# Experts in pairs: the second product in five whole token tiles instead of four whole and two half ones

## What is computed

```
capacity = max(1, int(N / E * K * CAP_FACTOR))          # 2048 / 32 * 4 * 1.25 = 320
buf = zeros((E + 1, capacity, d)).at[e_s, p_s].set(xf[tok])[:E]
h = silu(einsum('ecd,edh->ech', buf, wg)) * einsum('ecd,edh->ech', buf, wu)     # h: 256 inner
out_e = einsum('ech,ehd->ecd', h, wd)
routed = zeros_like(xf).at[tok].add(out_e[flat_e, pos] * gates)
```

## Time and profile before

| | us |
|---|---|
| median of 3 runs | 1134.17 (1133.24 to 1136.13) |
| span of the profiled execution | 1172.3 |
| second product of the experts (L1143), TensorE busy | 126.5 for the full tiles and half tiles together |
| first product (L1129, L1130), TensorE busy | 96.4 and 89.8 |
| expert stages, first to last pair's start | 150.1 to 287.8 and 998.6 to 1136.3 |

### The profile page before, as it was taken

How to read it: one execution, slowest core, us unless ns; L and a number is a source line. 1 busy time by engine, 2 the same in 40 slices (tenths; PEclk the granted TensorE clock), 3 DMA queues, 4 the chain that set the end, 5 groups by cost and what they waited for, 6 DMA issues and landing times.

```text
span 1172.3 us, 17171 instructions
## 1 busy us (share of the span) xinstructions
PE 972.9 (83%) x5887; PEld 752.4 (64%) x5887; DVE 548.8 (47%) x1503; ACT 356.1 (30%) x701; POOL 365.8 (31%) x550
## 2 busy tenths in 40 slices
PE   2305699999198999999999999999999653999994
PEld 1203366666134888979888498887999632666663
DVE  7533244444536674727273556362712541444444
ACT  2100122222023335343432443434353210222222
POOL 2736435555100311111110011444421073355551
PEclk9998899999579999999999999999999775999997
DMA  9400234453400000000000000101000002344435
GB/s 362 166 24 27 58 93 142 146 164 99 147 18 0 19 1 19 1 19 1 19 1 1 0 20 1 37 20 38 19 1 1 28 27 58 105 142 147 153 96 183
DMA packets 79285, 76.31 MB, mean 65 GB/s; under 512 B 10409, under 2 KB 69947, under 8 KB 78454
## 3 DMA queue, kind: packets, MB, share of 16 engines
q1 hardware_dynamic: 70006, 63.15, 17.3%
q0 software_dynamic: 9216, 12.33, 3.1%
HBM read 48.13 MB, written 30.21 MB: 67 GB/s over the span
## 4 chain that ended last, share of the span: by engine, by line
PE 72%; DVE 10%; issue 7%; another core or an unknown queue 6%; DMA 2%; ACT 2%; SPq 1%; POOL 1%; DVEq 0%; POOLq 0%; ACTq 0%
PE PS L1232 22%; PE PS L1143 8%; PE PS L1212 7%; PE PS L1129 6%; PE PS L1194 6%; PE PS L1130 5%; PE PS L1174 3%; PE PS L1283 3%; PE PS L1151 2%; PE PS L1197 1%; PE PS L1176 1%; PE PS L1109 1%; PE PS L1267 1%; DVE xs L899 1%
## 5 line engine op out<-in xcount | busy, mean ns | idle before, releaser
L1232 PE MATMUL PS<-area_v,pT 128*128 128x128 f32 x2304 | 316.5, 277 | 2.9 <-POOL pT L463 2.9
L1232 PEld LDWEIGHTS PS<-area_v,pT 128*128 128x128 f32 x2304 | 305.3, 192 | 13.3 <-POOL pT L463 3.0
L605 ACT ACTIVATE pT<-PS 128x512 f32<-128x512 f32 (+3 forms) x384 | 185.1, 490 | 250.6 <-PE PS L1212 244.8
L463 POOL TENSOR_SCALAR_AFFINE_SELECT pT<-pT 128x128 f32<-128x128 f32 x256 | 78.7, 311 | 469.4 <-ACT pT L605 468.3
L917 DVE TENSOR_REDUCE mxp<-PS 128x2 f32<-128x1024 f32 (+2 forms) x192 | 180.6, 955 | 83.0 <-PE PS L1197 62.2
L482 POOL DMA_INDIRECT ybuf<-area_o,yidx x160 | 155.4, 971 | 184.1 <-DVE area_o L876 143.3
L451 POOL DMA_INDIRECT xbuf<-xn,sidx x128 | 124.6, 974 | 130.6 <-DVE sidx L812 67.0
L1212 PE MATMUL PS<-Qc,Kz 128*128 128x512 f32 (+3 forms) x384 | 156.4, 411 | 7.8 <-ACT pT L605 5.3
L1143 PE MATMUL PS<-area_v,area_o 128*128 128x128 f32 (+1 forms) x768 | 126.5, 291 | 0.0
L1194 PE MATMUL PS<-Kz,Qn 128*128 128x512 f32 (+3 forms) x384 | 117.9, 389 | 4.1 <-DVE mxp L917 3.3
L1143 PEld LDWEIGHTS PS<-area_v,area_o 128*128 128x128 f32 (+1 forms) x768 | 93.9, 172 | 31.8 <-issue 11.3
(11 more groups left out here) (172 smaller groups left out, 945.1 us busy)
## 6 DMA issues: line engine op xcount, KB each, us to landing
area_v<-xbuf SPq DMA_DIRECT2D x32, 340.0 KB
area_v<-in_L_ffn_wg_dram SPq DMA_DIRECT2D x32, 256.0 KB
area_v<-in_L_ffn_wu_dram SPq DMA_DIRECT2D x32, 256.0 KB
area_v<-in_L_ffn_wd_dram SPq DMA_DIRECT2D x64, 128.0 KB
yg<-ybuf SPq DMA_DIRECT2D x24, 256.0 KB, 4.4
xbuf<-Kz SPq DMA_DIRECT2D x4, 1360.0 KB, 10.3
ybuf<-Kz SPq DMA_DIRECT2D x2, 2048.0 KB
Kz<-Kn SPq DMA_DIRECT2D x32, 128.0 KB
```

Of the source, the lines that this page charges most:

```text
L463: nc.gpsimd.affine_select(out=block_, in_=block_, pattern=[[1, P]], compare_op=ALU.is_ge, fill=zero, base=0, channel_multiplier=-1).then_i ...
L605: nc.scalar.activation(pT[:, N % 4, 0:w], PS[:, 4 + N % 2, 0:w], ACT.Exp).then_inc(exp_done, 1)
L1232: ins = mm(PS[:, 6 + half, (i % 4) * P:(i % 4 + 1) * P], pT[:, N % 4, k * P:(k + 1) * P], area_v[:, (j * NH + h) * VW:(j * NH + h) * VW + ...
```

## The change

The inner rows of both experts of a pair go into one buffer `hp`, 640 columns for each half c, the second expert's behind the first's. The second product runs over the five tiles of 128 columns of that buffer: tiles 0, 1 with the first expert's weights into bank 6, tile 2 with the first expert's weights into bank 6 and once more with the second's into bank 7, tiles 3, 4 with the second's into bank 7. Of tile 2's two results the copies take the upper 64 rows of the one and the lower 64 of the other, as before. Tiles are outside now, halves c inside. The turn of the next pair stands behind tiles 0 and 1 of the first expert; tile 2 waits for the inner rows of both experts. `y_ps` of the first expert is given behind its tile 2.

```diff
+        hp = area_o[:, 2 * HC * 512:2 * HC * 512 + HC * PAIR].rearrange("p (c n) -> p c n", c=HC)
...
-                            tt(hb[a][:, c, 0:CAP], sil[a][:, c, 0:CAP], PS[:, 4 + c, 0:CAP], ALU.mult)\
+                            tt(hp[:, c, a * CAP:(a + 1) * CAP], sil[a][:, c, 0:CAP], PS[:, 4 + c, 0:CAP], ALU.mult)\
                                 .then_inc(h_ready, 1)
...
                 pe.wait_ge(d_in[j], it * 32 + (32 * NPAIR // 2 * L + 32))
-                down(L, it, j, 0)
+                pe.wait_ge(y_sb, it * 4 + (2 * NPAIR * L + 2 * j + 1))
+                for t in range(2):
+                    down(L, it, j, 0, t)
                 if not (isinstance(it, int) and j):
                     turn(L, it + j, 1 - j)
-                down(L, it, j, 1)
+                down(L, it, j, 0, 2).then_inc(y_ps, 1)
+                pe.wait_ge(y_sb, it * 4 + (2 * NPAIR * L + 2 * j + 2))
+                for t in range(2, 4):
+                    down(L, it, j, 1, t)
+                down(L, it, j, 1, 4).then_inc(y_ps, 1)
...
-            def down(L, it, j, a):
-
-                pe.wait_ge(y_sb, it * 4 + (2 * NPAIR * L + 2 * j + a + 1))
-                tiles = ((0, P, 0, 0), (P, P, 0, 1), (2 * P, 64, 0, 2)) if a == 0 else \
-                    ((64, P, 0, 1), (64 + P, P, 0, 2), (0, 64, 64, 0))
-
+            def down(L, it, j, a, t):
+
+                first = t == 2 * a
+                bank, slot = 6 + a, t - 2 * a
                 for c in range(HC):
-
-                    pe.wait_ge(h_ready, it * 8 + (4 * NPAIR * L + 4 * j + 2 * a + c + 3))
-                    for n, (col, m, p0, t) in enumerate(tiles):
-                        ins = mm(PS[p0:p0 + m, 6 + a, t * D:(t + 1) * D], hb[a][:, c, col:col + m], wdt[j][:, a, c, :],
-                                 start=(c == 0 and n == 0) , stop=(c == HC - 1), skip_group_check=True)
-                ins.then_inc(y_ps, 1)
+                    if t in (0, 2) and a == t // 2:
+                        pe.wait_ge(h_ready, it * 8 + (4 * NPAIR * L + 4 * j + 2 * a + c + 3))
+                    elif t == 2:
+                        pe.wait_ge(h_ready, it * 8 + (4 * NPAIR * L + 4 * j + c + 5))
+                    ins = mm(PS[:, bank, slot * D:(slot + 1) * D], hp[:, c, t * P:(t + 1) * P], wdt[j][:, a, c, :],
+                             start=(first and c == 0), stop=(c == HC - 1), skip_group_check=True)
+                return ins
```

## The result

The changed kernel takes 1096.98 us (median of 4 runs, 1095.54 to 1099.3), the kernel before 1134.41 on the same chip: ratio 0.9676, with an interval of 0.9659 to 0.9693. A second measurement on another chip gives 1095.02 beside 1133.92, ratio 0.965 (0.9633 to 0.9668). The forecast was 1100.0, in a range from 1091 to 1112.

The account below looks back on a forecast made before the run. TensorE's pace was taken to bound the expert stages. A layer saves 1.20 + 7 x 1.15 + 7 x 1.10 + 0.2 = 17.2 us, both 34.3, off the median 1134.2: 1099.9, range 1091 to 1112.

Parts of the forecast that it names:

- Step 1: TensorE's second products fall from 3.81 to 2.66 us a pair, 1.15 less; the turn from 0.60 to 0.55.
- Rival D: Second products: full tiles cost more and the holes stay, 14 us slower, 1148; chance 0.02.
- Step 2: Next pair's start: 0.10 us goes on TensorE, but VectorE's later copies add 0.05 in odd, 0.10 in even pairs.
- Rival B: The experts' chain through VectorE has slack: 1.30 us saved a pair, 40 us, 1094; chance 0.10.
- Step 3: Middle tile's wait for both experts' inner rows: slack 0.5 us, no cost; some 0.3 us in a layer's last pair.
- Rival A: Middle tile's wait not free in some even pairs, where TensorE's report comes late: 7 us, 1107; chance 0.20.
- Step 4: First expert's results complete later, copies at about 6.8 us of the pair; GpSimd's scatters and DMA still fit, no cost.
- rival C: Some other queue (VectorE's moved copies, GpSimd) comes late: half of the gain lost, 1117; chance 0.06.
- Step 5: A layer's last pair ends in the scatters, not TensorE: only 0.2 us gained, its 1.2 us saving lost.
- The first pair: First pair of a layer: no index work of that kind behind copies, so 1.20 us less.
- The sum: Over both layers 34.3 us saved, taken unscaled off the median 1134.2: 1099.9; forecast as worked out has chance 0.60.

Follow-up runs that it names:

- Experiment 2: Kernel before with whole tiles alone: second expert's inner rows shifted 64 columns in their own buffer, order and waits unchanged; 1096.67 us, ratio 0.9667.
- Experiment 5: Changed kernel with the first expert's share of the middle tile ahead of the turn instead of behind it; 1103.46 us, ratio 0.9723.
- e_swap: Changed kernel with VectorE's two waits ahead of each expert's first multiply exchanged, on a chip where before takes 1171.61 us; 1156.57 us, ratio 0.9866.
- b_again: The kernel before, no edit, profiled again on a chip where it takes 1134; 1133.82 us in one run, span 1132.1 us.
- e_turn2: Kernel of Experiment 2 with the turn, and ScalarE's copy of it, moved between the experts' first products; 1086.25 us, ratio 0.9574.

## Why the prediction was right, and where its steps were off

**Step 1, TensorE's own work: right.** Forecast for the second products and the turn was 2.66 + 0.55 = 3.21 us a pair, measured 3.22. Experiment 2 shows that the shape alone does it. The mean of 0.158 us in the prediction hid what it consists of: 0.111 everywhere and four passages, 2 x 0.337 inside the experts and 2 x 0.30 at their ends, 1.27 a pair, of which 0.05 lies in the turn and 0.10 at the start of the next pair. Odd pairs are 1.29 shorter, 9.12 to 7.83. Rival D (full tiles cost more, 1148) needed more than 0.158 between full records, and they stand 0.111 apart.

**Step 2, the next pair's start: wrong in sign.** It put +0.05 us on odd and +0.10 on even pairs for the copies that come later. The copies did come 0.09 later. But a pair's first part became 2.35 and 2.49 us where 2.50 and 2.67 were forecast, 0.10 and 0.08 shorter than before. In odd pairs the chain was misread: ScalarE's result binds there, and it comes 0.10 earlier behind a whole tile. The odd row had the hint, an idle time of 0.28 us ahead of the multiply. In even pairs the chain was read rightly, and the shift along it was not: it was carried through the index work unchanged, but 0.09 of it vanished in the operations that end with GpSimd's scatter, and the last index operation became 0.06 shorter, since the scatters stand otherwise beside it. The step had no term for either. Rival B gave the other sign ("-0.10 instead"), for slack in VectorE's work; that holds in odd pairs, while in even ones the -0.08 came by a way that nobody had forecast. Its 1094 lies as far below the 1097 as the forecast above. In all it is 7 x 0.14 + 7 x 0.17 = 2.2 us a layer.

**Step 3, the new wait: right.** No gap shows ahead of the middle tile in the 30 pairs that have a turn; in the last pair of each layer two records stand 0.21 apart, 0.2 us where the step said some 0.3. Experiment 5 gives the price of the other place, 6.5 to 8.4 us over the two medians of the changed kernel. Rival A priced late reports at 7 us through this wait. They exist, as its rows suggested, but not on the other chips, whatever the kernel. Where they were seen, they cost the changed kernel's relatives 10 to 22 us in the pairs, and in e_swap's pair above through the copies of y and not through the middle tile.

**Step 4, copies and scatters: right.** The first expert's copies start at 6.69 and 6.83 (forecast 6.8), GpSimd is 57% busy, TensorE's records follow each other through the second products, and no loss of the size of rival C (1117) is left to explain.

**Step 5, the last pair: right in kind, small.** It still ends in the scatters. The end of the first layer's experts, against the earlier trace rows:

```profile
248.79 0.97 POOL L483 DMA_INDIRECT ybuf<-area_o,yidx  x1 [1.40 <-DVE area_o L877]
...
253.90 0.97 POOL L483 DMA_INDIRECT ybuf<-area_o,yidx  x1 [0.30 <-issue]
```

The last pair starts at 240.98, so its first scatter comes 7.81 us into it, where b_again has 8.19: 0.38 us and not 0.2. **The first pair** was priced at 1.20 saved. It takes 10.79 and 11.04 us before and 10.46 and 9.83 after, so it saved 0.33 and 1.21: it does not run at the full clock, with a granted share of 0.83 and 0.82 before and 0.72 and 0.79 after. In the execution that the prediction read it had the full clock and took 9.12.

**The sum.** 34.3 us forecast, 38.3 between the spans: 2 x 2.2 from step 2, 2 x 0.18 from step 5, less 0.9 in the first pairs, make 38.2. So the two misses partly cancel, and the larger of them is step 2. Taking the saved time off the median and not off the profiled span was right, since the 38 us by which that span exceeds it did not come back on other chips; they lie ahead of the first pair and between the layers.

## What to carry to other kernels

- A stage bound by TensorE's own record spacing gains by what stands between records, not by columns. Group the records by form, and where a smaller tile is not faster look at the distances where the form changes. Then ask how many passages between forms there are rather than how many small tiles; putting the half tiles together brought 21 of the 37 us by a changed loop order alone.
- When a chain moves later, follow the shift through each operation to the point where it is to bind. An operation that ends together with something else swallows it. And an idle time ahead of the instruction on the path says that its own engine may not be what bound it; whether its start moves with the end of the one or the other chain, over many repetitions and several kernels, decides.
- A fixed job that depends on nothing nearby (here the turn) belongs where the engine stands waiting, not where it is convenient. That was worth 8.8 us, a quarter of the change itself.

## What the runs showed of the hardware that I had not expected

- Going from full weight tiles (128 columns) to half ones (64) and back costs 0.30 to 0.34 us in fp32 a time, whether two or four half records lie between; half records among themselves run 0.109 us apart, full ones 0.111.
- VectorE's index operations (128x5, and the 128x20 behind it) that run into the end of one of GpSimd's scatters finish within 0.01 us of that end, and the first takes 0.24 to 0.37 us instead of 0.17; in the middle of a scatter they take 0.17. A 128x5 operation behind whose start a scatter starts within 0.04 us takes 0.20 to 0.24 and ends 0.20 behind the scatter's start. VectorE's multiplies out of PSUM keep their 0.49 beside scatters.
- One kernel differs by 37 us between two chips (1134 and 1171), another, that of e_turn2, by 68 us (1086 and 1154.5). A ratio measured on one of them does not hold on the other: 0.957 and 0.986. Some 39 to 44 us of that are lost outside the pairs, by the kernel before and its relatives alike. What seems to lose more are kernels whose TensorE reports fall near the end of a row of scatters; that was read from the traces and not tried.
